# Context loads moved to ScalarE's queue, maxima planned 20 ahead instead of 12, and one LoRA slot more

## The chip, the cores and the metric

One Trainium2 chip, one of its cores. The metric is the device time of one execution in microseconds (us), lower is better. TensorE is called PE, VectorE DVE, ScalarE ACT, GpSimd POOL and SyncE SP, as in the profile's rows; PEld is PE's weight load.

## What is computed

Two cross-attention layers, one after the other, over the same context. `B` = 4 sequences, 256 query rows of width 512, 1601 context rows of width 512, 32 heads of 16.

```python
# layer 0: weights W + 2 A B (LoRA, rank 16); 8 key/value heads, each shared by 4 query heads
q = lora(x, Wq, Aq, Bq); k = lora(ctx, Wk, Ak, Bk); v = lora(ctx, Wv, Av, Bv)
attn = softmax(q @ k.T / 4); x = x + lora(attn @ v, Wo, Ao, Bo)
# layer 1: 32 key/value heads, biases, a mask over the context rows, layernorm behind
q = x @ Wq.T + bq; k = ctx @ Wk.T + bk; v = ctx @ Wv.T + bv
attn = softmax(where(mask, q @ k.T / 4, -inf)); x = x + (attn @ v) @ Wo.T + bo
out = (x - mean) / sqrt(var + 1e-5) * ln_g + ln_b
```

## The kernel before

The attention is cut into 64 **units** of four heads of one sequence: units 0 to 31 are layer 0 (8 for each sequence), 32 to 63 layer 1. One unit is scored in 13 steps of 124 context rows, each step in two halves (two heads each). A half is a matmul on PE into one of two score banks (line 929 in layer 0, 934, two matmuls, in layer 1), then an exponential on ACT (line 1028) into one of 12 places of `p_sb`. The values (line 952) are multiplied in bursts of three to five steps.

The softmax is shifted by each row's maximum, and this maximum is found *before* the scores: for each unit PE makes 32 further score chunks ("max", line 909) into a ring of three banks and DVE reduces each to one column (line 1130). `collect` joins them, PE turns them ("turn m", line 916), DVE copies them (line 1151), and SP writes them with four small DMAs as two extra rows for each half into `q_stack` (line 1398). The scores of the unit wait for these rows. With the rows in place the score matmul subtracts the maximum itself.

The keys come by way of DRAM. A k product (line 840) is read by ACT, split in two parts by POOL (1256, 1258), written to `k_dram` by SP (1361). A **stack** is then read from `k_dram` into one of three slots of `k_stack` with six DMAs of 200 KB (line 1383), in layer 1 with two more for the mask row (1389). In layer 0 two units share a stack (16 of them), in layer 1 each unit has its own (32). A stack for unit u + 2 may be read when the unit that used its slot is scored. Maxima and scores of a unit both wait for its whole stack (`stack_ready`).

The context of a sequence lies in `ctx_sb` in four chunks (three of 992 KB, one of 226 KB). When the last product that uses a chunk is done, SP loads that chunk of the next sequence (line 1302): 4 loads at the start and 28 later.

The order of everything is written out by a planner, the class `Plan`, before the instructions are made: one list of steps, which each engine goes through in order, taking the steps that are its own. The planner keeps modelled times of PE, DVE and ACT (none for DMAs). What sets the order around the change:

- `lag` says how far the maxima are behind their target, which is `LEAD` chunks ahead of the scores:

```python
lag = CHUNKS * (1 + (s + half / 2) / NT) + self.LEAD - sum(self.max_at)
rows = [h for h in (0, 1) if self.max_open(h, 2 if lag > 0 else 1)]
```

with CHUNKS = 32 and NT = 13. With lag > 0 and a free bank in the ring, a maximum goes first of all. `max_open` lets the maxima of unit u + 2 begin while u is scored only if lag > 0, its stack step has been emitted and its queries are turned ("turn q", line 897).
- `enter_unit(u)` emits what must be done before unit u: the k product of u + 2, then (once "turn m" of u is out) the step `stack` for u + 2, then the q product.
- SP's queue takes its steps in the planner's order. A step that waits holds back all behind it.
- `norm` emits one step of the layernorm for each score step: `sums`, `variance`, `root` (a square root on ACT, line 1074, which needs another function table), `centre`, `inverse`, `normalise`.

The start: LoRA factors of k and q lie in two slots (on `att_t` and `att`); those of v and o follow in the same slots when the first are used up ("fold", PE line 823, DVE 1091). `wo` and the o factors are issued by SP after the first stack.

Of the kernel before, what the change touches and what calls it, by code (L numbers as in the profile page):

```python
# [22 lines left out]
class Plan:  # L23
# [4 lines left out]
    def __init__(self, B, UB, QT, KT, NT, CT, NC, NM, CHUNKS, LEAD, RING, chunks_of_keys):  # L28
# [25 lines left out]
        self.todo, self.writes = [], []  # L54
# [39 lines left out]
    def read(self):  # L94
# [27 lines left out]
        else:  # L122
# [156 lines left out]
    def turn(self, entry):  # L279
# [37 lines left out]
    def prologue(self):  # L317
# [7 lines left out]
        self.step("load w", "wo")  # L325
        self.step("load lora", "o")
# [50 lines left out]
    def ready(self, entry):  # L377
# [88 lines left out]
    def load_stack(self):  # L466

        self.step("stack", self.next_stack)
        self.stacked, self.next_stack = self.next_stack, None

    def score(self, s, half):
        u, i = divmod(s, self.NT)
        n = 2 * s + half
        self.enter("half", half, self.score_free[n % 2])
# [6 lines left out]
        self.write_keys(s)  # L481

# [29 lines left out]
    def main(self):  # L512
        NT, CHUNKS = self.NT, self.CHUNKS
        total, s, half, places = self.UNITS * NT, 0, 0, 6
        while self.values_done < total:
# [10 lines left out]
            score_wait = max(0.0, self.score_free[(2 * s + half) % 2] - self.begins("half", half)) if score else None  # L526
# [60 lines left out]
    NORM = {"sums": 950, "variance": 200, "root": 0, "centre": 620, "inverse": 200, "normalise": 620}  # L587
# [8 lines left out]
def cross_attention_pair(nc, x, xT, ctxT, mask, w0, w1, out):  # L596
    B, S, H = x.shape
    T = ctxT.shape[2]
    P = 128
# [29 lines left out]
    LEAD = 12  # L629
# [41 lines left out]
    with ctx:  # L671
# [40 lines left out]
        lora_a = att_t[0:RANK, :, :].rearrange("p k s -> p (k s)")  # L712
        lora_b = att[0:RANK, :, :].rearrange("p q h -> p (q h)")
# [28 lines left out]
        s_w = {n: sem(f"s_w_{n}") for n in ("a0", "b0", "a1", "b1", "wq", "wk0", "wv0", "wo", "wk1", "wv1", "wq1", "wo1",  # L742
# [6 lines left out]
        s_m = [sem(f"s_m{i}") for i in range(3)]  # L749
# [14 lines left out]
        lora_slot = {"k": 0, "q": 1, "v": 0, "o": 1}  # L764
# [36 lines left out]
        def lora_loaded(e, n):  # L801
            s = lora_slot[n]
            e.wait_ge(s_w[f"a{s}"], 16 if n in "kq" else 32)
            e.wait_ge(s_w[f"b{s}"], 16 if n in "kq" else 32)
# [10 lines left out]
        def tensor(engine):  # L815
            e = Once(engine)
            for kind, *a in steps:
                if kind == "fold":
# [5 lines left out]
                                  lora_a[:, s * H + k * P:s * H + (k + 1) * P], lora_b[:, s * H:s * H + w],  # L824
# [94 lines left out]
                elif kind == "score":  # L919
# [6 lines left out]
                    e.wait_ge(s_m[u % 3], 64 * (u // 3 + 1))  # L926
# [85 lines left out]

        def scalar(engine):
            e = Once(engine)
            for kind, *a in steps:
                if kind == "score":
# [5 lines left out]
                    else:  # L1022
# [53 lines left out]
        def vector(engine):  # L1076
# [8 lines left out]
            for kind, *a in steps:  # L1085
# [32 lines left out]
                elif kind == "read turn q":  # L1118
# [4 lines left out]
                    if u >= 3:  # L1123
                        e.wait_ge(s_m[u % 3], 64 * (u // 3))
# [21 lines left out]
                elif kind == "read turn m":  # L1146
                    u, = a
                    e.wait_ge(s_made["turn m"], u + 1)
                    if u >= 2:
                        e.wait_ge(s_m[(u - 2) % 3], 64 * ((u - 2) // 3 + 1))  # L1150
# [136 lines left out]
        def sync(engine):  # L1287
            e = Once(engine)

            def load_lora(n):  # L1290
                s = lora_slot[n]
                if n in "vo":
                    e.wait_ge(s_made["fold"], fold_count["k" if n == "v" else "q"])
                engine.dma_start(lora_a[:, s * H:(s + 1) * H], w0[f"A{n}T"]).then_inc(s_w[f"a{s}"], 16)
                engine.dma_start(lora_b[:, s * H:s * H + widths[n]], w0[f"B{n}"]).then_inc(s_w[f"b{s}"], 16)

            def load_ctx(z, c):
                lo, hi = chunk(c)
                user = plan.ctx_after.get((z, c))
                if user is not None:  # L1300
                    e.wait_ge(s_made[user[0]], made[user])
# [146 lines left out]
```

## Time and profile before

| | us |
|---|---|
| median of 3 runs | 1794.33 |
| lowest, highest | 1787.55, 1794.78 |
| the profiled execution | 1788.64 |
| its span, first to last instruction | 1786.9 |
| mean granted clock of TensorE | 0.972 of full speed |

The span is the profiled execution less 1.7 us around it. Busy times are unions of an engine's instructions; on PE, where matmuls are pipelined, an interval counts as busy when any matmul is under way. A row of the form "A <- B" in a list of waits is idle time of A that ended when B finished.

### The profile page before, as it was taken

The numbers are of one execution on the slowest core, as the hardware profiler recorded it, in microseconds if no ns is written. First come the engines' busy times: TensorE is split into PE (matmuls) and PEld (weight loads), VectorE is DVE, ScalarE is ACT, GpSimd is POOL, SyncE is SP. The second block draws the span as 40 slices with busy tenths as digits, with TensorE's granted clock in tenths as the row PEclk, the third lists the DMA queues.
The fourth block names the chain that finished last, engine by engine and source line by source line (L and its number), as shares of the span: only waits on it lengthen the run. The fifth ranks groups of instructions, "written<-read, shape, count | busy, mean of one in ns | idle before, by whom it ended". The sixth has DMA issues, their size and how long they took to land.

```text
span 1786.9 us, 43754 instructions
## 1 busy us (share of the span) xinstructions
PE 1696.2 (95%) x18340; PEld 1193.5 (67%) x18340; DVE 1256.7 (70%) x2743; ACT 1022.5 (57%) x1896; POOL 176.3 (10%) x260
## 2 busy tenths in 40 slices
PE   6799999999999999999999999998999989999996
PEld 4566666676656766665667777776777677777663
DVE  2667776777758788776765776776777767777661
ACT  0056665666656666665655655665666656666554
POOL 2010121102120001121201100000000000000000
PEclk9799999999999999999999999999999999999997
DMA  8832335212353222224433444442554245344310
GB/s 203 234 81 48 66 84 151 48 32 72 84 151 66 30 48 62 63 84 125 101 42 77 85 80 106 58 58 42 104 86 57 38 64 118 44 59 58 46 25 13
DMA packets 65029, 138.12 MB, mean 77 GB/s; under 512 B 12540, under 2 KB 49436, under 8 KB 64832
## 3 DMA queue, kind: packets, MB, share of 16 engines
q1 hardware_dynamic: 64832, 135.33, 37.6%
q8 instruction: 144, 2.36, 0.6%
q14 instruction: 53, 0.43, 0.1%
HBM read 97.84 MB, written 34.89 MB: 74 GB/s over the span
## 4 chain that ended last, share of the span: by engine, by line
PE 86%; DMA 5%; DVE 3%; ACT 2%; SPq 2%; issue 1%; POOL 0%; DVEq 0%; ACTq 0%; POOLq 0%
PE value L952 21%; PE ring L909 13%; PE work L840 12%; PE work L860 11%; PE score L934 8%; PE score L929 8%; PE work L885 3%; PE work L990 3%; DMA k_stack<-k_dram 2%; PE ring L897 2%; PE work L868 1%; DVE chunk_max L1130 1%; ACT p_sb L1028 1%; DMA ctx_sb<-ctxT 1%; PE ring L962 1%
## 5 line engine op out<-in xcount | busy, mean ns | idle before, releaser
L1028 ACT ACTIVATE p_sb<-score 124x512 f32<-124x512 f32 (+1 forms) x1664 | 931.8, 598 | 639.8 <-PE score L934 317.7
L1130 DVE TENSOR_REDUCE chunk_max<-ring 128x1 f32<-128x402 f32 x2048 | 1055.8, 569 | 202.3 <-PE ring L909 187.8
L909 PE MATMUL ring<-k_stack,q_stack 64*128 64x402 f32 x2048 | 780.6, 454 | 16.3 <-DMA k_stack<-k_dram 10.5
L952 PE MATMUL value<-p_sb,v_sb 124*32 124x256 f32 x6656 | 422.5, 389 | 0.2 <-ACT p_sb L1028 0.2
L909 PEld LDWEIGHTS ring<-k_stack,q_stack 64*128 64x128 f32 x2048 | 356.9, 188 | 86.4 <-DVE chunk_max L1130 32.3
L934 PE MATMUL score<-q_stack,k_stack 64*124 64x256 f32 (+1 forms) x1664 | 362.3, 324 | 23.8 <-DMA q_stack<-few_rows 15.4
L929 PE MATMUL score<-q_stack,k_stack 64*124 64x512 f32 (+1 forms) x832 | 381.3, 503 | 1.9 <-ACT p_sb L1028 1.5
L860 PE MATMUL work<-wv,ctx_sb 64*124 64x128 f32 x3840 | 371.3, 278 | 3.1 <-issue 1.6
L860 PEld LDWEIGHTS work<-wv,ctx_sb 64*124 64x124 f32 x3840 | 341.2, 185 | 13.3 <-PE work L860 7.1
L840 PE MATMUL work<-ctx_sb,wk 64*128 64x402 f32 x1280 | 309.2, 518 | 6.2 <-DMA ctx_sb<-ctxT 4.9
L952 PEld LDWEIGHTS value<-p_sb,v_sb 124*32 124x32 f32 x6656 | 190.9, 111 | 160.7 <-issue 54.0
L934 PEld LDWEIGHTS score<-q_stack,k_stack 64*124 64x124 f32 (+1 forms) x1664 | 238.9, 184 | 79.6 <-ACT p_sb L1028 32.6
L929 PEld LDWEIGHTS score<-q_stack,k_stack 64*124 64x124 f32 (+1 forms) x832 | 144.3, 183 | 78.7 <-ACT p_sb L1028 42.7
L840 PEld LDWEIGHTS work<-ctx_sb,wk 64*128 64x128 f32 x1280 | 150.4, 189 | 31.0 <-issue 9.4
L1256 POOL CAST k_parts<-full 128x402 fp32r<-128x402 f32 x80 | 41.6, 520 | 634.8 <-ACT full L1039 623.3
L1267 POOL CAST q_nat<-full 128x512 fp32r<-128x512 f32 x32 | 19.7, 617 | 824.5 <-DVE full L1115 666.5
L885 PE MATMUL work<-wq,xt_sb 64*128 64x128 f32 x1024 | 94.3, 290 | 5.3 <-ACT v_sb L1050 2.1
L885 PEld LDWEIGHTS work<-wq,xt_sb 64*128 64x128 f32 x1024 | 81.7, 193 | 16.1 <-PE work L885 6.8
L1125 DVE CAST q_stack<-ring 128x512 fp32r<-128x512 f32 x64 | 44.0, 689 | 50.8 <-PE ring L897 48.5
L990 PE MATMUL work<-wo,att_t 64*128 64x512 f32 x256 | 77.8, 624 | 0.8 <-ACT att_t L1060 0.6
L1258 POOL TENSOR_TENSOR k_parts<-full,k_parts 128x402 fp32r<-128x402 f32 x80 | 77.3, 966 | 6.4
L1050 ACT ACTIVATE v_sb<-work 124x512 f32<-124x512 f32 (+2 forms) x100 | 38.4, 455 | 58.1 <-PE work L860 48.8
(66 smaller groups left out, 553.4 us busy)
## 6 DMA issues: line engine op xcount, KB each, us to landing
k_stack<-k_dram SPq DMA_DIRECT2D x288, 200.1 KB
k_dram<-k_parts SPq DMA_DIRECT2D x60, 402.0 KB, 2.7
ctx_sb<-ctxT SPq DMA_DIRECT2D x24, 992.0 KB, 6.9
k_dram<-k_parts SPq DMA_DIRECT2D x20, 395.0 KB, 3.3
q_stack<-few_rows SPq DMA_DIRECT2D x256, 2.0 KB
wq<-l_Wq SPq DMA_DIRECT2D x2, 1024.0 KB, 12.7
xt_sb<-xT SPq DMA_DIRECT2D x4, 512.0 KB, 13.0
wo<-l_Wo SPq DMA_DIRECT2D x2, 1024.0 KB, 9.0
```

Of the source, the lines that this page charges most:

```text
L840: done = engine.matmul(work[:, n, 0:MW], w[rows, k, col * P:(col + 1) * P], ctx_sb[rows, k, lo:lo + MW], start=(p == 0), stop=(p == 2 * KT ...
L860: done = engine.matmul(work[0:TT, n, j * P:(j + 1) * P], ctx_sb[rows, k, t0:t0 + TT], w[rows, k, col * P:(col + 1) * P], start=(p == 0), s ...
L885: done = engine.matmul(work[:, n, 0:P], xt_sb[rows, z % 2, k, n * P:(n + 1) * P], wq[rows, k, col * P:(col + 1) * P], start=(p == 0), stop ...
L909: engine.matmul(ring[bank_of["max", u, half, m]][:, 0:MW], q_stack[rows, u % 3, j, q * P:(q + 1) * P], k_stack[rows, 2 * (z % 3) + (u % 2 ...
L929: engine.matmul(score_bank[n % 2][0:tn, :], k_stack[rows, slot + u % 2, t0:t0 + tn], q_stack[rows, u % 3, :, :].rearrange("p j q -> p (j q)"),
L934: done = engine.matmul(score_bank[n % 2][0:tn, j * S:(j + 1) * S], k_stack[rows, slot + j, t0:t0 + tn], q_stack[rows, u % 3, j, :], start= ...
L952: done = engine.matmul(value_bank[32 * j:32 * j + 32, 0:S], v_sb[0:tn, seq % 2, i, head * VW:head * VW + 32], p_sb[0:tn, (2 * n + j % 2) % ...
L990: done = engine.matmul(work[:, n, :], att_t[rows, k, n * P:(n + 1) * P], wo[rows, k, :], start=(p == 0), stop=(p == 2 * KT - 1))
L1028: engine.activation(p_sb[0:tn, n % PLACES, :], score_bank[n % 2][0:tn, :], ACT.Exp, scale=SCALE).then_inc(s_exp, 1)
L1125: engine.tensor_copy(q_stack[:, u % 3, :, :].rearrange("d j q -> d (j q)"), ring[bank_of["turn q", u]][:, :]).then_inc(s_taken["turn q"], 1)
L1130: engine.tensor_reduce(chunk_max[:, u % 2, half, m // NM, m % NM:m % NM + 1], ring[bank_of["max", u, half, m]][:, 0:MW], AX.X, ALU.max)\
L1258: engine.tensor_tensor(dst[:, 1, :], one, dst[:, 0, :], ALU.subtract).then_inc(s_part, 1)
```

## The change

- **Loads of the context.** The 28 later loads are issued by ACT instead of SP, with the same wait. The planner collects them and emits them at the end of `load_stack`, or after a score when no stack is outstanding. The products on a new chunk are allowed 4 score steps after the load's step, not 2. The planner counts 450 ns of ACT for each chunk.
- **Loads of the start.** The o factors get a slot of their own in `xt_sb` (second half), and they and `wo` are issued before the constant rows and the mask; the load of `xt` 1 now waits for the fold of o.
- **Maxima.** `LEAD` is 20, not 12. The planner holds the scores of a unit back until 4.5 us after its "turn m". The semaphore of the rows is split by half: a score waits for its own half's two DMAs.
- **Root.** The step `root` comes after `centre` instead of ahead of it, and two empty steps stand between it and `inverse`.

```diff
@@ Plan.read @@
-                self.slow += [("variance", b), ("root", b)]
-                self.slow += [("centre", b, r) for r in range(self.QT)] + [("inverse", b)]
+                self.slow += [("variance", b)] + [("centre", b, r) for r in range(self.QT)]
+                self.slow += [("root", b), ("time",), ("time",), ("inverse", b)]
@@ Plan.done @@
-                    self.ctx_now[c], self.ctx_since[c] = z + 1, self.now
-                    self.step("load ctx", z + 1, c)
+                    self.ctx_now[c], self.ctx_since[c] = z + 1, None
+                    self.ctx_loads.append((z + 1, c))
+                    self.scalar_free += 450
@@ Plan.turn @@
+        if kind == "turn m":
+            self.rows_at[name[1]] = max(self.vector_free, end + self.HOP) + 4500
@@ Plan.prologue @@
-        self.step("load w", "wo")
-        self.step("load lora", "o")
@@ Plan.ready @@
-            return all(self.ctx_now[c] == z and (z == 0 or self.ctx_since[c] + 2 <= self.now) for c in chunks)
+            return all(self.ctx_now[c] == z and (z == 0 or self.ctx_since[c] is not None and self.ctx_since[c] + 4 <= self.now) for c in chunks)
@@ Plan.load_stack @@
         self.step("stack", self.next_stack)
         self.stacked, self.next_stack = self.next_stack, None
+        self.load_ctx()
+
+    def load_ctx(self):
+        for z, c in self.ctx_loads:
+            self.step("load ctx", z, c)
+            self.ctx_since[c] = self.now
+        self.ctx_loads = []
@@ Plan.score @@
-        self.enter("half", half, self.score_free[n % 2])
+        self.enter("half", half, max(self.score_free[n % 2], self.rows_at[u]))
...
         self.write_keys(s)
+        if self.next_stack is None:
+            self.load_ctx()
@@ Plan.main @@
-            score_wait = max(0.0, self.score_free[(2 * s + half) % 2] - self.begins("half", half)) if score else None
+            score_wait = max(0.0, max(self.score_free[(2 * s + half) % 2], self.rows_at[u]) -
+                             self.begins("half", half)) if score else None
@@ cross_attention_pair @@
-    LEAD = 12
+    LEAD = 20
...
+        lora_a.append(xt_sb[0:RANK, 1, 0:2, :].rearrange("p k s -> p (k s)"))
+        lora_b.append(xt_sb[0:RANK, 1, 2:4, :].rearrange("p k s -> p (k s)"))
...
-        s_m = [sem(f"s_m{i}") for i in range(3)]
+        s_m = [[sem(f"s_m{i}{half}") for half in range(2)] for i in range(3)]
...
-        lora_slot = {"k": 0, "q": 1, "v": 0, "o": 1}
+        lora_slot = {"k": 0, "q": 1, "v": 0, "o": 2}
@@ tensor, score @@
-                    e.wait_ge(s_m[u % 3], 64 * (u // 3 + 1))
+                    e.wait_ge(s_m[u % 3][half], 32 * (u // 3 + 1))
@@ scalar @@
+                elif kind == "load ctx":
+
+                    z, c = a
+                    user = plan.ctx_after[z, c]
+                    e.wait_ge(s_made[user[0]], made[user])
+                    load_ctx(engine, z, c)
@@ sync @@
             def load_xt(b):
+                if b == 1:
+                    e.wait_ge(s_made["fold"], fold_count["o"])
...
             engine.dma_start(wv0[:, :, :], by_tile(w0["Wv"])).then_inc(s_w["wv0"], 16)
+            load_lora("o")
+            engine.dma_start(wo[:, :, :], by_tile(w0["Wo"])).then_inc(s_w["wo"], 16)
             e.wait_ge(s_x_rows, X_ROWS)
```

## Rows read from the trace of the kernel before

**Rows 1.** The page: busy time (share of the span), and granted clock in 40 slices
```profile
PE 1696.2 (95%) x18340; PEld 1193.5 (67%) x18340; DVE 1256.7 (70%) x2743; ACT 1022.5 (57%) x1896; POOL 176.3 (10%) x260
...
PEclk9799999999999999999999999999999999999997
```

**Rows 2.** The waits, longest in total: who <- for whom: us, times, longest
```profile
PE score L934 <- DMA q_stack<-few_rows: 15.4, 7, 3.9
...
PE ring L909 <- DMA k_stack<-k_dram: 10.5, 3, 3.8
...
ACT rstd L1074 <- DVE rstd L1202: 6.2, 1, 6.2
...
PE work L840 <- DMA ctx_sb<-ctxT: 4.9, 3, 2.7
```

**Rows 3.** The timeline of the start: start, duration, engine, line [idle before <- releaser]
```profile
39.97 2.67 SPq L1383 DMA_DIRECT2D k_stack<-k_dram  x6
...
42.68 0.42 SPq L1338 DMA_DIRECT2D wo<-l_Wo  x1
...
55.42 7.16 PE L823 MATMUL work<-att,att_t 16*128 16x512 f32 x8 [10.32 <-DMA att<-l_Bo]
...
62.51 1.04 PE L909 MATMUL ring<-k_stack,q_stack 64*128 64x402 f32 x3
```

**Rows 4.** The timeline at the first change of sequence
```profile
289.51 1.54 SPq L1302 DMA_DIRECT2D ctx_sb<-ctxT  x3
...
293.26 4.75 SPq L1383 DMA_DIRECT2D k_stack<-k_dram  x6
...
310.63 0.67 PE L909 MATMUL ring<-k_stack,q_stack 64*128 64x402 f32 x1 [3.60 <-DMA k_stack<-k_dram]
```

**Rows 5.** Windows: length, busy PE, PEld, DVE, ACT, POOL, granted clock, DMA share, GB/s
```profile
56.00:68.00 12.00, 11.67 (x51) 6.51 (x51) 6.73 (x12) 0.00 (x0) 0.00 (x0) 0.53 1.05 387
...
300.00:310.00 10.00, 7.02 (x72) 4.44 (x68) 5.33 (x13) 3.90 (x7) 0.00 (x0) 0.98 1.05 165
...
820.00:830.00 10.00, 8.69 (x74) 5.26 (x74) 5.84 (x14) 3.97 (x7) 0.00 (x0) 0.83 0.28 92
...
1030.00:1040.00 10.00, 8.68 (x108) 6.03 (x109) 5.06 (x11) 4.42 (x10) 1.26 (x2) 1.00 0.18 35
...
1220.00:1230.00 10.00, 8.02 (x81) 7.41 (x82) 5.29 (x11) 7.44 (x11) 0.00 (x0) 0.66 0.87 125
```

**Rows 6.** The timeline of unit 55's first half: SP's stack, a burst of values
```profile
1538.70 2.65 SPq L1383 DMA_DIRECT2D k_stack<-k_dram  x6
...
1547.12 2.37 PE L952 MATMUL value<-p_sb,v_sb 124*32 124x256 f32 x40
```

**Rows 7.** Windows of one us, columns as in Rows 5: the DMA share falls to nothing
```profile
1547.00:1548.00 1.00, 1.00 (x19) 0.55 (x20) 0.99 (x3) 0.73 (x2) 0.00 (x0) 1.00 0.95 128
...
1549.00:1550.00 1.00, 1.00 (x16) 0.42 (x7) 0.11 (x1) 0.00 (x0) 0.00 (x0) 1.00 0.03 6
1550.00:1551.00 1.00, 1.00 (x15) 1.00 (x14) 0.95 (x4) 0.68 (x2) 0.00 (x0) 1.00 0.00 0
```

**Rows 8.** Maxima (line 909 alone) begun up to a time: PE's count, then PEld's
```profile
0.00:1540.10 1540.10, 694.56 (x1805) 315.90 (x1805) 0.98 0.40 83
0.00:1547.10 1547.10, 698.71 (x1818) 318.04 (x1818) 0.98 0.40 83
...
0.00:1554.30 1554.30, 701.02 (x1825) 319.17 (x1825) 0.98 0.40 83
```

**Rows 9.** The chain at unit 33's end: start, duration, what
```profile
950.50 0.37 SPq L1383
...
954.00 9.64 DMA k_stack<-few_rows
...
963.78 0.38 PE ring L909
```

**Rows 10.** The instructions that touch `ctx_sb`: ns min/median/max, first and last start
```profile
L1302 SPq DMA_DIRECT2D ctx_sb<-ctxT x32: 368/502/1905, 2.1 to 1510.2; - x32
```

**Rows 11.** The groups by line: busy us, mean ns, idle before, releaser
```profile
L1028 ACT ACTIVATE p_sb<-score 124x512 f32<-124x512 f32 (+1 forms) x1664 | 931.8, 598 | 639.8 <-PE score L934 317.7
```

More of the change, by code:

```diff
@@ L53, in __init__ @@
         self.ctx_now, self.ctx_since, self.chunk_product = [0] * NC, [0] * NC, [None] * NC
-        self.todo, self.writes = [], []
+        self.rows_at = {}
+        self.todo, self.writes, self.ctx_loads = [], [], []
         self.stacked, self.next_stack = 1, None
@@ L585, in main @@
         assert not self.todo and self.current is None
-    NORM = {"sums": 950, "variance": 200, "root": 0, "centre": 620, "inverse": 200, "normalise": 620}
+    NORM = {"sums": 950, "variance": 200, "root": 0, "time": 0, "centre": 620, "inverse": 200, "normalise": 620}
     def norm(self):
@@ L711, in cross_attention_pair @@
         rstd = sb("rstd", [P, QT])
-        lora_a = att_t[0:RANK, :, :].rearrange("p k s -> p (k s)")
-        lora_b = att[0:RANK, :, :].rearrange("p q h -> p (q h)")
+        lora_a = [att_t[0:RANK, 2 * i:2 * i + 2, :].rearrange("p k s -> p (k s)") for i in range(2)]
+        lora_b = [att[0:RANK, i, :] for i in range(2)]
+        lora_a.append(xt_sb[0:RANK, 1, 0:2, :].rearrange("p k s -> p (k s)"))
+        lora_b.append(xt_sb[0:RANK, 1, 2:4, :].rearrange("p k s -> p (k s)"))
         mask_rows = p_sb[0:B, 0:4, :].rearrange("p a n -> p (a n)")[:, 0:T].bitcast(I32)
@@ L740, in cross_attention_pair @@
         s_x_rows = sem("s_x_rows")
-        s_w = {n: sem(f"s_w_{n}") for n in ("a0", "b0", "a1", "b1", "wq", "wk0", "wv0", "wo", "wk1", "wv1", "wq1", "wo1",
+        s_w = {n: sem(f"s_w_{n}") for n in ("a0", "b0", "a1", "b1", "a2", "b2", "wq", "wk0", "wv0", "wo", "wk1", "wv1", "wq1", "wo1",
                                             "rows", "cols", "mask", "x")}
@@ L802, in lora_loaded @@
             s = lora_slot[n]
-            e.wait_ge(s_w[f"a{s}"], 16 if n in "kq" else 32)
-            e.wait_ge(s_w[f"b{s}"], 16 if n in "kq" else 32)
+            e.wait_ge(s_w[f"a{s}"], 32 if n == "v" else 16)
+            e.wait_ge(s_w[f"b{s}"], 32 if n == "v" else 16)
             e.wait_ge(s_w[{"k": "wk0", "q": "wq", "v": "wv0", "o": "wo"}[n]], 16)
@@ L823, in tensor @@
                     engine.matmul(work[:, bank_of["fold", n, k], 0:w],
-                                  lora_a[:, s * H + k * P:s * H + (k + 1) * P], lora_b[:, s * H:s * H + w],
+                                  lora_a[s][:, k * P:(k + 1) * P], lora_b[s][:, 0:w],
                                   start=True, stop=True).then_inc(s_made["fold"], 1)
@@ L1011, in tensor, with load_ctx @@
                     done.then_inc(s_made["turn mask"], 1)
+        def load_ctx(engine, z, c):
+            lo, hi = chunk(c)
+            engine.dma_start(ctx_sb[:, :, lo:hi], ctxT[z % B].rearrange("(k p) t -> p k t", p=P)[:, :, lo:hi])\
+                .then_inc(s_ctx[c], 16)
         def scalar(engine):
@@ L1123, in vector @@
                     if u >= 3:
-                        e.wait_ge(s_m[u % 3], 64 * (u // 3))
+                        for half in range(2):
+                            e.wait_ge(s_m[u % 3][half], 32 * (u // 3))
                     engine.tensor_copy(q_stack[:, u % 3, :, :].rearrange("d j q -> d (j q)"),
@@ L1149, in vector @@
                     if u >= 2:
-                        e.wait_ge(s_m[(u - 2) % 3], 64 * ((u - 2) // 3 + 1))
+                        for half in range(2):
+                            e.wait_ge(s_m[(u - 2) % 3][half], 32 * ((u - 2) // 3 + 1))
                     engine.tensor_copy(m_turned[:, u % 2, :], ring[bank_of["turn m", u]][0:2 * ROWS, 0:P])\
@@ L1291, in load_lora @@
                 s = lora_slot[n]
[L1292 to L1301, printed above, removed]
-                engine.dma_start(ctx_sb[:, :, lo:hi], ctxT[z % B].rearrange("(k p) t -> p k t", p=P)[:, :, lo:hi])\
-                    .then_inc(s_ctx[c], 16)
+                if n == "v":
+                    e.wait_ge(s_made["fold"], fold_count["k"])
+                engine.dma_start(lora_a[s], w0[f"A{n}T"]).then_inc(s_w[f"a{s}"], 16)
+                engine.dma_start(lora_b[s][:, 0:widths[n]], w0[f"B{n}"]).then_inc(s_w[f"b{s}"], 16)
             def load_xt(b):
+                if b == 1:
+                    e.wait_ge(s_made["fold"], fold_count["o"])
                 if b >= 2:
@@ L1313, in sync @@
             for c in range(NC):
-                load_ctx(0, c)
+                load_ctx(engine, 0, c)
             load_lora("q")
@@ L1336, in sync @@
                     load_lora(a[0])
-                elif kind == "load w":
-                    engine.dma_start(wo[:, :, :], by_tile(w0["Wo"])).then_inc(s_w["wo"], 16)
                 elif kind == "load layer 1":
@@ L1352, in sync @@
                     engine.dma_start(wq[:, :, :], by_tile(w1["Wq"])).then_inc(s_w["wq1"], 16)
-                elif kind == "load ctx":
-                    load_ctx(*a)
                 elif kind == "load xt":
@@ L1398, in sync @@
                             engine.dma_start(raw(q_stack[at:at + 1, u % 3, :, :]).rearrange("o j (q n) -> o (j q) n", n=P),
-                                             raw(m_turned[of:of + ROWS // 2, u % 2, :])).then_inc(s_m[u % 3], 16)
+                                             raw(m_turned[of:of + ROWS // 2, u % 2, :])).then_inc(s_m[u % 3][half], 16)
                 elif kind == "normalise":
```

## The prediction

> **What bounds the kernel now.** I read the page first: TensorE is busy for 1696 us of 1787, DVE for 70% and ACT for 57% [rows 1]. So the time is PE's work at the clock it is granted, plus PE's idle time; an edit gains only by taking idle time from PE or by sparing it a drop of the clock. Then the list of waits, for where PE idles: 10.5 us in three waits for a stack read from `k_dram`, 15.4 us in seven waits of the first score of a unit for its rows of maxima, 4.9 us for context chunks [rows 2]. Then the timeline of the start, where PE idles 10.3 us for the o factors and `wo`, issued behind the first stack [rows 3]. Last, windows around each idle stretch: after it the granted clock is at its lower level (1.2 GHz) for a while. A window of 10 us at 0.66 has lost 3.4 us of full-speed time, one at 0.83 1.7 us, and after 1.3 us of idling at 1037 us nothing was lost [rows 5]. I counted five drops of the first size and two of the second behind the waits for stacks and rows: 5 x 3.4 + 2 x 1.7 = 20.4 us.
>
> **What the change takes away.**
>
> - *Start.* `wo` and the o factors go ahead of the constant rows. The fold of o then runs right after the mask's turn at 45 us and no longer ends at 62.5. What is late next is the first stack: issued at 39.97, and a stack takes about 12 us (below), so it landed near 52; the 1 MB moved ahead of it delays SP by some 2.7 us (1 MB at the 387 GB/s that the loads behind the start reach [rows 5]), so 54.6. The first maximum began at 62.51 [rows 3]: gain 8 us. The load of `xt` 1 waits for the fold of o, but is wanted only in unit 6 or so, 150 us later: nothing. Bounds 4 and 11.
> - *Rows.* With LEAD 20 the maxima of a unit are ready 8 chunks earlier, 8/32 of a unit of some 27 us (1787 less 60 for the start, over 64) = 6.8 us. The longest wait for rows is 3.9 us [rows 2], so all 15.4 us go. The semaphore by halves then gains nothing more: the rows are there.
> - *Stacks behind the context.* At the change of sequence SP issues three chunks at 289.5, two writes, then the stack at 293.26; PE wants it at 307.0 and gets it at 310.63 [rows 4]. Three such waits, 10.5 us, plus 1.6 us in layer 1 for a stack that came behind late writes: 12.1 us.
> - *Context.* The second pair of chunks no longer stands behind a stack in SP's queue: 2.7 of the 4.9 us.
> - *Clock.* The 20.4 us above, as these waits go.
>
> Together 8 + 15.4 + 12.1 + 2.7 + 20.4 = 59 us.
>
> **What costs nothing.** The root waited for DVE once, 6.2 us, at the very end of the kernel [rows 2], where DVE's order does not change and the wait stays; in the middle it holds ACT for its two table loads wherever it stands. The empty steps issue nothing.
>
> **What it adds.**
>
> - *ACT.* 28 issues of 0.37 to 0.51 us, once 1.9 us under a full queue [rows 10]: 14 us of ACT. ACT is idle for 640 us before its exponentials, mostly waiting for PE's scores [rows 11]; this hides the most part. But an issue in front of an exponential delays the bank that the next score wants. I take 4 us; bounds 0 and 14.
> - *A new wait, for the stack.* This is the large term. A stack of layer 1 is issued when the last scores of the unit before are done, 1538.70 in unit 55's case [rows 6]; neither LEAD nor the empty queue can bring that forward. Its bytes move until 1549 to 1550 [rows 7]. Where PE waited for one, from the issue at 950.50 (or a little before) to the maximum at 963.78 it took 13 us [rows 9]; I use 12. The planner has no time for DMAs and holds a stack for ready as soon as it is emitted. Now the maxima. Unit 57's first is the 1825th, 32 x 57 + 1, and it began just ahead of 1554.3, 3.5 us after its stack landed. When unit 55 began, 1805 were out: 32 x 56 + 13, so the lead of 12 holds on the chip [rows 8]. With 20, the same place in the order is reached 8 maxima earlier, where the 1817th stood: the 1818th had begun by 1547.1 [rows 8]. By the formula of `lag` too, unit u + 2 opens 13 x (1 - 20/32) = 4.9 steps into unit u instead of 8.1. So the first maximum of 57 is issued at about 1547, ahead of the burst of values at 1547.12 [rows 6], and PE stands until 1550.5: a wait of 3.5 us. If the planner puts the burst first, 0.7 us. If "turn q" of unit u + 2 comes late (in about half of the units it is emitted only with that burst), the maximum is held back anyway and waits 0 to 2 us. I take 2 us a stack, between 0.7 and 3.5, and 25 of layer 1's 32 stacks (those that were already slack because of a wait for rows, and the last, are left out): 50 us.
> - *Layer 0.* Here a slot is free long before, and SP issues the stack right behind the rows, which come 6.8 us earlier too; nothing changes. Only the stacks behind key writes or a context load don't move: I count 7 at 2 us, 14 us. The three at the changes of sequence are among them: without the chunks ahead of it the stack would land at 293.3 + 12 = 305, and the maximum that came at 307.0 would come at about 300 were its queries turned by then.
> - *Clock again.* 32 waits of about 2 us. Waits of 1.3 to 3.6 us lost 0, 1.7 or 3.4 us each [rows 5]. I take 1.7 us for 12 of them: 20 us; bounds 0 and 54 (all at 1.7).
>
> Together 4 + 50 + 14 + 20 = 88 us.
>
> The Trainium skill bears on one point. In the windows at the change of sequence the DMA engines' share is 1.05 while only 165 GB/s move [rows 5], so a stack fills all of them. "DMA: Bandwidth & Descriptors", in "Issuing engines are not separate DMA queues", says that transfers issued by ScalarE run on the same DMA engines as SP's and interleave with them. The trace fits the first half and has no transfer from ScalarE to show the second. By that rule chunks in flight slow a stack beside them instead of standing ahead of it, and the landing at 305 would be 307 or later; that would lie inside my 2 us a stack.
>
> **The sum.** 88 - 59 = +29 us on the profiled execution's 1788.6 us: 1817.6. That execution is 5.7 us under the median of the runs but inside their range (1787.6 to 1794.8), so I keep it as the base and predict 1817 us, 1.3% above the median. Differences under 0.5%, 9 us, I count as none: 1785 to 1803.
>
> **Rivals.**
>
> 1. *The stacks come in time, and the kernel is faster.* The first maximum of u + 2 is held back by something that moves less than LEAD: the turn of its queries, a busy ring bank, the burst of values put first. For it: the 1818th maximum had begun by 1547.1 but no other by 1550.1, three microseconds in which the landing nearly catches up [rows 7, 8]. Against it: in the planner a maximum with lag > 0 goes before everything. With 32 new waits of 0.5 us and no drop of the clock: 16 + 4 - 59 = -39, and with the start at its best 1747; I put it at 1755. It decides when the new waits with their clock stay under 46 us, 1.4 us a stack.
> 2. *An even trade.* 1.6 us a stack and 8 drops: 51 + 14 + 4 - 59 = +10, or less: 1790 to 1800. For it: all terms are of one size.
> 3. *The maxima wait in full.* 3.5 us at each of 32 stacks and 1.7 us of clock for each, 166 us, + 4 - 59 = +111: 1900. Against it: the units whose queries are turned late.
> 4. *ACT becomes the wait.* If ACT's issue blocks as SP's did under a full queue, 28 x 1.9 = 53 us on ACT, of which perhaps 20 reach PE: the forecast plus 16, 1833. Its queue would hold only its own four chunks, which speaks against it.
>
> **How the numbers follow.** Forecast 0.48; rival 1 0.24; rival 2 0.18; rivals 3 and 4 0.05 each. The forecast's own range is 1803 to 1845 (1.3 to 2.7 us a stack, less or more of the clock). The range for 8 in 10 must take in both signs: 1758 to 1850. Slower by over 0.5%: the forecast, 3 and 4, 0.57. Within 0.5%: 0.19, most of rival 2. Faster: 0.24.
>
> **What the profile of the changed kernel would show.** The start: the fold of o from about 45 us, the first maximum at about 54.6. The list of waits: no `q_stack<-few_rows` on PE; and, if I am right, PE ring L909 <- DMA k_stack (from `k_dram`, or `few_rows` in layer 1, whose mask rows are issued last) some 30 times and 50 to 80 us in total, each at 5 steps into a unit. Fewer than 10 such waits, or under 20 us, and the forecast is wrong and rival 1 right. The page's PEclk row would have more 9s turned to 8s in layer 1. DMA queues: a second hardware queue with the chunks. ACT's table loads for the root stay. The prediction falls if the planner's order, with its new times, puts bursts or products in front of the first maximum of u + 2; that I could only judge from the order before.

## The result, and the profile after

The changed kernel takes 1832.53 us (median of 4 runs, 1826.42 to 1834.03), the kernel before 1794.55 beside it: a ratio of 1.0211, 95% interval 1.0173 to 1.0249, so slower by 2.1%. The forecast was 1817 us and slower, within a range of 1758 to 1850.

The page after, the parts that answer to [rows 1], with the DMA queues and the start of the chain that ended last:

```profile
PE 1708.1 (93%) x18340; PEld 1208.7 (66%) x18340; DVE 1257.8 (69%) x2743; ACT 1022.5 (56%) x1896; POOL 175.8 (10%) x260
...
PEclk8799999999999999999998999989999999999988
...
q1 hardware_dynamic: 50048, 112.38, 32.0%
q10 hardware_dynamic: 14784, 22.95, 4.3%
...
PE 78%; DMA 12%; SPq 4%; ACT 2%; DVE 2%; issue 1%; POOL 0%; ACTq 0%; DVEq 0%; POOLq 0%
```

The span is 1832.0 us and the mean granted clock 0.961, against 1786.9 and 0.972. The same 18340 matmuls keep PE busy for 12 us more, and PE is idle for 1832.0 - 1708.1 = 123.9 us instead of 90.7. The two 8s in the middle of the PEclk row stand in slices with long waits for a stack; the 8s at its ends are the start and the end of the kernel. DMA has 12% of the chain, where it had 5%. The new queue q10 carries the context chunks issued by ACT.

The list of waits after, which answers to [rows 2] (line 924 is the old 909, line 1100 the old 1074):

```profile
PE ring L924 <- DMA k_stack<-few_rows: 55.2, 19, 7.7
PE ring L924 <- DMA k_stack<-k_dram: 15.2, 3, 5.9
...
ACT rstd L1100 <- DVE rstd L1230: 6.2, 1, 6.2
...
PE work L855 <- DMA ctx_sb<-ctxT: 2.0, 1, 2.0
```

The waits of the scores for their rows (15.4 us in seven) are gone. In their place the first maximum of a unit waits for its stack: 70.4 us in 22 waits, where it was 12.1 in four.

The timeline after, at units 33 and 41, each with SP's stack and the first maximum that needs it (35 x 32 = 1120 maxima had begun by 967.7, 43 x 32 = 1376 by 1197.5, so these are the first of units 35 and 43; line 1403 is the old 1383):

```profile
952.97 1.78 SPq L1381 DMA_DIRECT2D k_dram<-k_parts  x2
954.80 3.06 SPq L1403 DMA_DIRECT2D k_stack<-k_dram  x6
957.90 1.23 SPq L1409 DMA_DIRECT2D k_stack<-few_rows  x2
967.83 0.71 PE L924 MATMUL ring<-k_stack,q_stack 64*128 64x402 f32 x2 [6.88 <-DMA k_stack<-few_rows]
...
1185.51 2.65 SPq L1403 DMA_DIRECT2D k_stack<-k_dram  x6
...
1197.64 0.67 PE L924 MATMUL ring<-k_stack,q_stack 64*128 64x402 f32 x1 [3.58 <-DMA k_stack<-few_rows]
```

From SP's issue to the maximum 12.1 us pass at the second, 13.0 at the first, as in [rows 9]. The wait is the part of this in which PE had nothing else in front: 3.58 us for a plain stack, and 6.88 where two key writes stand before the stack in SP's queue. Nine waits of 3.3 us and more hold 43.9 of the 55.2 us. The 22 maxima that waited came 11.6 to 13.0 us after their stack's issue in 18 cases (median 11.9) and 17.2 to 17.9 us after it in four; beside those four, context chunks were in flight.

The chain for the longest wait, at unit 45's first steps:

```profile
1301.13 0.31 SPq L1403
...
1304.63 13.51 DMA k_stack<-few_rows
...
1318.28 0.67 PE ring L924
```

Here the stack needs 17.1 us. ACT issued two context chunks of 992 KB at 1300.78 and 1301.19, just as SP began with it. Windows after, behind such waits (columns as in [rows 5]):

```profile
894.00:914.00 20.00, 15.20 (x184) 11.66 (x174) 8.56 (x22) 6.82 (x13) 0.00 (x0) 0.83 0.27 33
958.00:978.00 20.00, 13.12 (x151) 9.57 (x153) 7.12 (x19) 4.25 (x8) 0.00 (x0) 0.74 0.38 48
...
1192.00:1212.00 20.00, 16.42 (x176) 11.05 (x173) 10.15 (x25) 8.19 (x18) 0.00 (x0) 0.83 0.18 23
1223.00:1243.00 20.00, 16.74 (x172) 11.40 (x169) 12.17 (x29) 8.47 (x16) 0.00 (x0) 0.91 0.20 25
```

After each of the nine long waits the clock is at its lower level (1.2 GHz) for a stretch. In such windows of 20 us, one around each, the granted clock is 0.83 six times (20 x 0.17 = 3.4 us lost), 0.91 twice (1.8) and 0.74 once (5.2): 29 us together. By the intervals of the clock in the trace, 7 of the 29 us fell while PE still stood in the wait, the rest on matmuls behind it.

The start after, which answers to [rows 3], and the first change of sequence, [rows 4]:

```profile
43.18 2.67 SPq L1403 DMA_DIRECT2D k_stack<-k_dram  x6
...
49.04 0.59 PE L1024 MATMUL ring<-ident,p_sb 13*124 13x13 f32 x4 [1.60 <-DVE p_sb L1124]
49.48 7.17 PE L838 MATMUL work<-xt_sb 16*128 16x512 f32 x8
...
56.58 1.04 PE L924 MATMUL ring<-k_stack,q_stack 64*128 64x402 f32 x3
...
282.32 0.53 ACTq L1030 DMA_DIRECT2D ctx_sb<-ctxT  x1
...
285.31 3.06 SPq L1403 DMA_DIRECT2D k_stack<-k_dram  x6
...
303.16 0.70 PE L924 MATMUL ring<-k_stack,q_stack 64*128 64x402 f32 x2 [4.22 <-DMA k_stack<-k_dram]
```

### The profile page after: what moved, and what is told of

It is laid out like the page before. It is cut to its first block, busy times and chain, and to the rows that moved or that the text cites. A ratio compares the mean times of both kernels' runs of the same rounds, so it can differ in the third digit from the quotient of the medians.

```text
span 1832.0 us, 43837 instructions
## 1 busy us (share of the span) xinstructions
PE 1708.1 (93%) x18340; PEld 1208.7 (66%) x18340; DVE 1257.8 (69%) x2743; ACT 1022.5 (56%) x1896; POOL 175.8 (10%) x260
## 4 chain that ended last, share of the span: by engine, by line
PE 78%; DMA 12%; SPq 4%; ACT 2%; DVE 2%; issue 1%; POOL 0%; ACTq 0%; DVEq 0%; POOLq 0%
PE value L967 19%; PE ring L924 12%; PE work L855 12%; PE work L875 10%; DMA k_stack<-few_rows 9%; PE score L944 8%; PE score L949 6%; PE work L900 3%; SPq L1403 3%; PE work L1005 2%; DMA k_stack<-k_dram 2%; PE work L883 2%; PE ring L912 1%; ACT p_sb L1048 1%; PE ring L977 1%
## 5 line engine op out<-in xcount | busy, mean ns | idle before, releaser
L924 PE MATMUL ring<-k_stack,q_stack 64*128 64x402 f32 x2048 | 784.1, 460 | 76.9 <-DMA k_stack<-few_rows 55.2
L967 PE MATMUL value<-p_sb,v_sb 124*32 124x256 f32 x6656 | 433.3, 395 | 0.4 <-ACT p_sb L1048 0.4
L875 PE MATMUL work<-wv,ctx_sb 64*124 64x128 f32 x3840 | 376.9, 279 | 1.1
L944 PE MATMUL score<-q_stack,k_stack 64*124 64x512 f32 (+1 forms) x832 | 374.3, 502 | 3.1 <-ACT p_sb L1048 2.5
L949 PE MATMUL score<-q_stack,k_stack 64*124 64x256 f32 (+1 forms) x1664 | 357.0, 318 | 11.0 <-ACT p_sb L1048 10.4
L855 PE MATMUL work<-ctx_sb,wk 64*128 64x402 f32 x1280 | 303.7, 516 | 3.2 <-DMA ctx_sb<-ctxT 2.0
L1152 DVE CAST q_stack<-ring 128x512 fp32r<-128x512 f32 x64 | 44.1, 690 | 52.1 <-PE ring L912 49.9
```

Source lines behind the costliest of these rows:

```text
L855: done = engine.matmul(work[:, n, 0:MW], w[rows, k, col * P:(col + 1) * P], ctx_sb[rows, k, lo:lo + MW], start=(p == 0), stop=(p == 2 * KT ...
L875: done = engine.matmul(work[0:TT, n, j * P:(j + 1) * P], ctx_sb[rows, k, t0:t0 + TT], w[rows, k, col * P:(col + 1) * P], start=(p == 0), s ...
L924: engine.matmul(ring[bank_of["max", u, half, m]][:, 0:MW], q_stack[rows, u % 3, j, q * P:(q + 1) * P], k_stack[rows, 2 * (z % 3) + (u % 2 ...
L944: engine.matmul(score_bank[n % 2][0:tn, :], k_stack[rows, slot + u % 2, t0:t0 + tn], q_stack[rows, u % 3, :, :].rearrange("p j q -> p (j q)"),
L949: done = engine.matmul(score_bank[n % 2][0:tn, j * S:(j + 1) * S], k_stack[rows, slot + j, t0:t0 + tn], q_stack[rows, u % 3, j, :], start= ...
L967: done = engine.matmul(value_bank[32 * j:32 * j + 32, 0:S], v_sb[0:tn, seq % 2, i, head * VW:head * VW + 32], p_sb[0:tn, (2 * n + j % 2) % ...
```

## The experiments

Each ratio is to runs of the kernel before on the same chip; these had medians of 1788 to 1795 us. "Stack waits" are PE's waits for `k_stack` in the list of waits; "idle" is the span less PE's busy time; "clock" is (1 - mean granted clock) x span, both of the one profiled execution; "planned" is the median time from a stack's step to the unit's first maximum in the planner's own times. The clock's loss varies between executions of one kernel: in 43 of the kernel before it was 44 to 72 us (median 59), in the four of the changed kernel 62 to 71 (median 68). So a difference of 10 us in the clock's column tells nothing by itself, and the 50.0 of the kernel before is at the low side.

| kernel | planned | stack waits | idle | clock | us | ratio, 95% |
|---|---|---|---|---|---|---|
| before | 15.4 | 12.1 (4) | 90.7 | 50.0 | 1794.55 | 1 |
| changed | 11.1 | 70.4 (22) | 123.9 | 71.4 | 1832.53 | 1.0211 [1.0173, 1.0249] |
| changed, LEAD 12 | 15.7 | 10.4 (4) | 66.8 | 29.8 | 1762.41 | 0.9841 [0.9799, 0.9884] |
| changed, LEAD 15 | 13.4 | 24.8 (8) | 75.5 | 37.3 | 1785.91 | 0.9964 [0.9936, 0.9993] |
| before, LEAD 20 | | 80.2 (27) | 141.6 | 70.2 | 1849.23 | 1.0326 [1.0277, 1.0375] |
| changed, short stacks | 11.1 | 17.9 (10) | 73.7 | 37.0 | 1759.37 | 0.9830 [0.9798, 0.9863] |
| changed, planner told | 13.1 | 22.0 (8) | 71.2 | 42.5 | 1770.76 | 0.9905 [0.9880, 0.9931] |
| changed, chunks by SP | 11.1 | 64.3 (22) | 128.3 | 67.8 | 1835.85 | 1.0258 [1.0220, 1.0295] |
| changed, LEAD 12, chunks late | | 10.8 (4) | 79.2 | 47.9 | 1774.38 | 0.9927 [0.9900, 0.9954] |
| before, start alone | 15.4 | 9.3 (4) | 74.4 | 56.8 | 1784.85 | 0.9975 [0.9953, 0.9996] |
| before, chunks by ACT | 15.4 | 3.2 (3) | 82.6 | 42.6 | 1780.00 | 0.9960 [0.9937, 0.9983] |
| before, rows' plan | | 8.9 (3) | 67.6 | 35.1 | 1756.99 | 0.9836 [0.9811, 0.9861] |
| before, the three | 15.9 | 1.8 (2) | 63.6 | 29.7 | 1753.30 | 0.9815 [0.9783, 0.9846] |
| the three, LEAD 14 | 14.1 | 10.4 (6) | 75.7 | 40.6 | 1768.88 | 0.9888 [0.9857, 0.9920] |

**LEAD taken back, and LEAD alone.** Two kernels: `LEAD = 12` in the changed one, and `LEAD = 20` in the kernel before.

> The changed kernel with LEAD back at 12, all else kept. My theory (maxima planned 20 ahead come to a stack before it has landed): the waits of PE for k_stack fall from 70 us in 22 to under 12 us, the clock drops behind them go, and with the start's 8 us and the planner's wait for the rows kept the time is 1755 to 1775 us. Rival (the loss comes from ACT issuing the context's loads, or from the planner holding scores and products back): LEAD gives back little, 1810 us or more.

> The kernel before with LEAD 20 and nothing else. My theory: the waits for the rows of maxima (15 us) go, some 20 new waits for k_stack come, 60 us and more with the three at the changes of sequence, and the time is 1825 to 1850 us, above even the changed kernel, since the start's gain is missing. Rival (the loss needs the other edits): at most 1795 us.

The waits with LEAD 12 in the changed kernel, then with LEAD 20 in the kernel before:

```profile
PE ring L924 <- DMA k_stack<-k_dram: 10.4, 4, 3.6
...
PE score L944 <- DMA q_stack<-few_rows: 1.2, 1, 1.2
```
```profile
PE ring L909 <- DMA k_stack<-few_rows: 54.1, 21, 6.7
PE ring L909 <- DMA k_stack<-k_dram: 26.1, 6, 6.7
```

Both came out as expected. LEAD turns a gain of 1.6% into a loss of 2.1%, and alone costs 3.3%. In the first pair LEAD is the only difference, and no other wait of PE for a transfer changed by more than 1.2 us.

**Short stacks.** If the wait is for bytes, fewer bytes must shorten it, with LEAD left at 20. From the fourth stack on, this kernel issues 4 of a stack's 6 loads. The last third of its rows isn't read again, so that part of each product with the keys is computed from an earlier stack's.

```diff
-                    for r, part in KPARTS:
+                    for r, part in (KPARTS if z < 3 else KPARTS[0:2]):
```

> The changed kernel, LEAD 20, but from the fourth stack on only four of its six DMAs are issued (the second copy of the keys' upper part is left as it was, so the scores lack a small correction). The order of all engines is the same. A stack then lands about 3.5 us sooner (a third of 10 us of transfer). My theory: the waits for k_stack of 1 to 4 us go almost all, the four long ones of 6 to 8 us shrink to 3 or 4, together from 70 to 20 us or less, and the time is 1765 to 1790 us. Rival (the waits named k_stack only stand for another lag, as the queries' turn or DVE): the time falls by less than 10 us.

```profile
PE ring L924 <- DMA k_stack<-few_rows: 13.0, 7, 4.5
...
PE ring L924 <- DMA k_stack<-k_dram: 4.9, 3, 2.3
```

The order of the instructions is the changed kernel's, and the waits fall from 70.4 to 17.9 us, by 52.5. The time falls by 73 us, to 1759, just under the 1765 to 1790 that I expected. In the profiled spans, 72.3 us apart, 50.2 are idle time of PE and 23.7 are clock lost while PE was busy (53.7 and 30.0 us). The whole loss of the clock differs by 71.4 - 37.0 = 34.4 us; what of it falls in PE's idle time is idle time already.

**The planner told of the landing.** Loads and LEAD as in the changed kernel; the planner takes a stack as landed 12.5 us after its step and puts no maximum of that unit before it.

```diff
@@ Plan.load_stack @@
+        self.stack_at[self.next_stack] = max(self.free) + 12500
@@ Plan.maximum @@
-        self.enter("half", half, self.ring_free[bank])
+        self.enter("half", half, max(self.ring_free[bank], self.arrives(unit)))
```

> The changed kernel with LEAD 20 as it is, but the planner is told that a stack has landed 12.5 us after its step, and emits no maximum of the unit (and sets the time of none) before that, doing other work instead. Nothing else is changed; DMAs and their count are those of the changed kernel. Theory: LEAD 20 costs only through maxima that stand at the head of PE's queue before their stack is there; with them held back in the plan, the waits for few_rows fall from 55 to under 15 us and the time to 1760 to 1785. Rival: PE has nothing else to do in that time (scores held by ACT), so the idle time comes back under another name, p_sb or ring, and the time stays above 1810.

```profile
PE ring L930 <- DMA k_stack<-k_dram: 16.8, 5, 5.0
...
PE ring L930 <- DMA k_stack<-few_rows: 5.2, 3, 2.3
```

The waits for `few_rows` fell from 55.2 to 5.2 us and did not return under another name: idle time is 71.2 us. So PE had other work to put in front. The `k_dram` waits stayed; three of the five are at the changes of sequence, where PE had the stack 16.9 to 17.5 us after its issue, while the planner is told 12.5.

**Dose.** LEAD 15 in the changed kernel, with the two kernels of three edits further down.

> The changed kernel with LEAD 15, between the 12 and the 20 that were measured (1762 and 1832). In the planner's times the first maximum follows its stack's step by at least 9.5 us (median 13.4). Theory: the wait opens when this falls under about 12 us, so a part of the stacks is waited for, 10 to 25 us of waits for few_rows, time 1770 to 1795. Rival, that the time goes with LEAD in a straight line for another reason: 1762 + 70 x 3/8 = 1788 with hardly any waits for the stack.

```profile
PE ring L924 <- DMA k_stack<-k_dram: 17.1, 5, 4.7
PE ring L924 <- DMA k_stack<-few_rows: 7.7, 3, 3.9
```

The time fits both theories, the waits only the first: 24.8 us of them. But most are in layer 0 (`k_dram`), where I had expected `few_rows`. Waits of 10.4, 24.8 and 70.4 us at LEAD 12, 15 and 20 go with a planned distance of 15.7, 13.4 and 11.1 us, against the 11.6 to 13.0 us (17.2 to 17.9 beside context chunks) that a waited-for stack took in the changed kernel. With LEAD 15, 11.5 of the 24.8 us are at the three changes of sequence.

**Who issues the chunks.** In the changed kernel the 28 loads go back to SP at the places of the plan; in the kernel before they go to ACT at their old places.

> The changed kernel with the 28 later context loads issued by SP again, at the same place in the planner's order (behind the stack). If ACT's issues cost PE what I estimated, 4 us is gained; SP's queue then holds rows or stacks back by 0.5 us each, so the same time within 10 us: 1825 to 1840. Rival (ACT's issues are a large part of the loss): 1810 or less. Rival (a queue of its own is what keeps the stacks from being worse): 1845 or more.

> The kernel before with the 28 later context loads issued by ScalarE at the same places in the planner's order, nothing else. My reading: the stack at a change of sequence no longer stands behind three chunks in SP's queue but shares the DMA engines with them, so the three waits of 3.6 us shrink but do not go, and ACT's issues cost up to 4 us: the time is lower by 0 to 10 us. Rival (the queue was the cause): the three waits go wholly, 20 us with their clock. Rival (ACT's issues cost PE time): slower by 5 us or more.

The first changed nothing in the time that can be told, but two terms under it moved, against each other. At 97 us PE waits 9.8 us for a chunk, since all four now stand behind the second stack in SP's queue; the waits at the changes of sequence shrink from 15.2 to 11.0 us:

```profile
PE work L855 <- DMA ctx_sb<-ctxT: 12.0, 2, 9.8
```

The `few_rows` waits are 53.3 us in 19. The longest is again at unit 45, with the chunks issued by SP just ahead of the stack:

```profile
1304.89 2.97 SPq L1402 DMA_DIRECT2D k_stack<-k_dram  x6
...
1321.67 0.67 PE L924 MATMUL ring<-k_stack,q_stack 64*128 64x402 f32 x1 [7.80 <-DMA k_stack<-few_rows]
```

That is 16.8 us from issue to use, against 17.1 with ACT as the issuer. The Trainium skill, "DMA: Bandwidth & Descriptors", section "Issuing engines are not separate DMA queues", says that transfers of all issuers share the same DMA engines and interleave; the two figures agree. At the changes of sequence the issuer shows a little: PE had the stack 17.2 to 17.9 us after its issue with ACT as the chunks' issuer and 15.4 to 16.7 with SP, and the chunk issued last before the first of these stacks took 20.3 us instead of 9.1. In the kernel before, with its plan kept, the move helped a little, 0.4%:

```profile
PE ring L909 <- DMA k_stack<-k_dram: 1.9, 2, 1.2
```

There 10.5 us of waits became 1.9, where I had expected them to shrink less:

```profile
288.08 1.49 ACTq L1015 DMA_DIRECT2D ctx_sb<-ctxT  x3
...
290.75 0.94 PE L885 MATMUL work<-wq,xt_sb 64*128 64x128 f32 x12 [1.33 <-ACT full L1049]
...
293.79 3.65 SPq L1383 DMA_DIRECT2D k_stack<-k_dram  x6
...
308.27 0.41 PE L909 MATMUL ring<-k_stack,q_stack 64*128 64x402 f32 x1 [1.17 <-DMA k_stack<-k_dram]
```

The stack was not issued earlier than in [rows 4]; the last of the three chunks was issued 4.7 us before it instead of 2.7, and the stack took 14.5 us instead of 17.4. ACT's issues have a price here: they stand in front of ACT's reading of a product, and PE waits for ACT at each of the three changes of sequence, 3.8 us in all. In the changed kernel none shows: PE's waits for `p_sb` are 10.4 us in 11 with either issuer.

**Chunks kept away from a stack.** Since two chunks beside a stack cost it 5 us, I held them until five steps after a stack's step, with LEAD 12; they are no longer issued right behind a stack either.

```diff
-        if self.next_stack is None:
+        if self.next_stack is None and (s < 5 or s >= self.stack_now + 5):
             self.load_ctx()
```

> The changed kernel with LEAD 12, with the context's loads held back until five score steps (about 10 us) after a stack's step, so that a chunk is not in flight with a stack. If sharing the DMA engines is what leaves the 10 us of waits for k_stack in the run with LEAD 12, they fall to under 3 us and the time is 5 to 15 us under that run's: 1748 to 1757 us. Rival (those waits come from the key writes and the queries' load beside the stack, or from the late issue): no difference, 1762 within 4.

```profile
PE score L943 <- ACT p_sb L1047: 7.1, 7, 5.9
...
PE work L854 <- DMA ctx_sb<-ctxT: 5.5, 2, 3.4
```

The time came out against my reading: the stack waits stayed (10.8 us in four), new waits for chunks and for ACT opened, and it is 12 us slower than LEAD 12 alone. But the edit does not do what it was made for. It holds a chunk back behind the last stack, not ahead of the next one, and there nothing moved:

```profile
289.36 0.93 ACTq L1029 DMA_DIRECT2D ctx_sb<-ctxT  x2
...
290.32 0.53 ACTq L1029 DMA_DIRECT2D ctx_sb<-ctxT  x1
...
293.45 3.76 SPq L1402 DMA_DIRECT2D k_stack<-k_dram  x6
...
310.76 0.70 PE L923 MATMUL ring<-k_stack,q_stack 64*128 64x402 f32 x2 [3.44 <-DMA k_stack<-k_dram]
```

The last chunk goes out 3.1 us before the stack, as with LEAD 12 alone, and the stack takes 17.3 us. So this run does not tell whether chunks in flight make these waits.

**The start alone.** The kernel before with the o factors' slot and the early loads.

> The kernel before with the loads of the start alone (wo and the o factors ahead of the constant rows, in a slot of their own). My term for it was a gain of 8 us, bounds 4 and 11. In the changed kernel the first maximum began about 6 us earlier, so 6 to 8 us: a ratio of 0.9955 to 0.9965. Rival (the gain is given back, since a DMA that starts earlier delays the first stacks or the context of the second sequence): no difference, within 3 us.

The first maximum began at 56.39 instead of 62.51, but the ratio shows only 0.25%, under the 0.35 to 0.45% that I expected, with an interval that reaches from 0.04 to 0.47%. In all traces the first maximum comes at 61.3 to 62.5 us with the old start and at 54.1 to 57.4 with the new one.

**The rows' plan alone.** The kernel before, LEAD 12, and only the planner's hold of 4.5 us behind "turn m".

```diff
+        if kind == "turn m":
+            self.rows_at[name[1]] = max(self.vector_free, end + self.HOP) + 4500
...
-        self.enter("half", half, self.score_free[n % 2])
+        self.enter("half", half, max(self.score_free[n % 2], self.rows_at[u]))
```

> The kernel before with one edit of the planner: the scores of a unit are held back until 4.5 us after its turn of the maxima, so that other work is put there. LEAD stays 12, the semaphore stays whole. My reading after the first runs: this alone takes the 15 us of waits for the rows and their clock drops (12 us) away, 1765 to 1775 us on a base of 1790. Rival (the work that fills the wait is missing later; the planner's own total grows by 5 us): 1780 or more. Rival (the maxima's lead is what takes the waits): no gain.

```profile
PE ring L913 <- DMA k_stack<-k_dram: 8.9, 3, 4.3
```

No wait for rows is left, at LEAD 12. This edit alone gives 1.6%, more than I expected (1757 us, not 1765 to 1775) and as much as the whole changed kernel with LEAD 12.

**The three together, and LEAD 14.** Rows' plan, start and chunks by ACT in the kernel before; then the same with LEAD 14.

> The kernel before with three edits that were measured alone: the planner holds a unit's scores until 4.5 us after its turn m, wo and the o factors are loaded first at the start, and the context is loaded from ACT at the places where SP loaded it. LEAD stays 12, the root stays where it was. Alone they gave ratios of 0.9836, 0.9975 and 0.9960. My theory (each removes another wait: rows, start, stacks at a change of sequence) lets them add up: 0.977, about 1748 us, with waits for k_stack under 5 us. The rival is that with the rows' wait gone PE comes to the changes of sequence at another point and the waits there open again, or that clock lost in one place is lost in another: then 1755 or more, no better than the plan of the rows alone.

> The same with LEAD 14. In the planner's times the first maximum of a unit then follows its stack's step by at least 11.5 us (median 14.1) instead of 12.8 (15.9). A stack takes about 12 us, so my theory expects almost no new waits: within 0.3% of the one with LEAD 12, at most 5 us of waits for few_rows. A rival in which LEAD itself costs, by more turmoil in the order of maxima and scores, expects 5 us or more above it without such waits.

PE's waits for transfers with LEAD 12, then the stack waits with LEAD 14:

```profile
PE work L827 <- DMA wk<-l_Wk: 4.8, 1, 4.8
...
PE score L938 <- DMA q_stack<-few_rows: 2.3, 1, 2.3
...
PE ring L913 <- DMA k_stack<-k_dram: 1.5, 1, 1.5
```
```profile
PE ring L913 <- DMA k_stack<-k_dram: 9.1, 5, 2.5
...
PE ring L913 <- DMA k_stack<-few_rows: 1.3, 1, 1.3
```

The three give 0.9815, the lowest ratio of the study, but its interval overlaps that of the rows' plan alone (0.9836), and the full sum of 0.977 was not reached. The waits named are nearly gone (1.8 us for stacks, one of 2.3 for rows), 7.5 us of the start too, yet the idle time fell from 67.6 to 63.6 us only: others opened, among them again three for ACT at the changes of sequence (4.0 us). Whether the three add at all stays open. LEAD 14 costs 0.7% and brings 8.6 us more of stack waits, nearly all in layer 0. I had expected almost none: I set about 12 us beside the shortest planned distance, 11.5 us, while PE had the six waited-for stacks 12.4 to 15.3 us after their issue. The idle time grew by 12.1 us.

## Why the prediction was right, and where it was mis-sized

**The mechanism was right.** A maximum planned 20 ahead of the scores stands at the head of PE's queue before its stack has landed. Taking LEAD back removes the waits, LEAD alone makes them, fewer bytes shorten them, and telling the planner of the landing avoids most of them, at the same LEAD.

**The size of the stack term.** I took 25 x 2 + 7 x 2 = 64 us. Measured are 70.4, so 58 net of the old 12.1, where I had 52; the waits are 22, not some 30. The sum is close, its parts are not. In layer 1 there are 19 waits of 2.9 us instead of 25 of 2: the longer plain ones are at my upper bound of 3.5 us (3.26 to 3.84), three behind key writes exceed it (4.80, 6.34, 6.88), as does the one beside context chunks (7.72), and 20 of the 32 units have about 1 us or none. Unit 57 itself, on which I worked out 3.5 us, waits 0.93. In layer 0 only the three changes of sequence wait, 5.1 us each; four of the seven that I counted don't.

**The changes of sequence.** I priced 12.1 us as gone and took 6 of them back as new waits. In fact they grew from 10.5 to 15.2 us. Moving the chunks to ACT did not take their bytes out of the stack's way: at the first one the stack was issued at 285.31, 8 us earlier than in [rows 4], but PE had it only at 303.16, 17.9 us later, where I had counted 12. In [rows 4] 17.4 us pass, so the stack is hardly slower than before; with LEAD 20 its first maximum is due sooner after the issue. Of the two readings that I set side by side there, the traces favour chunks in flight that slow a stack, at 5 us and more where I allowed 2: where PE waited for such a stack, 16.8 to 17.9 us passed from issue to use with the last chunk 2.7 to 3.1 us ahead (the kernel before and the changed one), 13.8 to 15.3 us with it 4.7 ahead (the chunks by ACT at their old places). No run kept the chunks away to show it.

**The clock.** This is the term that was mis-sized most. I let 20.4 us go and put 20 us back, a change of nothing: 1.7 us for 12 of 32 waits. In the trace the clock falls at 14 of the 22 waits and loses 43 us, 3 each; the nine long waits of layer 1 alone lost 29 us. Over the whole profiled executions the loss went from 50.0 to 71.4 us, 21 more; between the medians of the executions (59 and 68) it is only 9 more, so how much of the 21 belongs to the change stays open. The profiled execution that I took as the base lost less than most and is 5.7 us under the median: from median to median the change is +38, where I had +29.

**The start.** I said 8 us; the first maximum came 5.9 earlier (56.58 for 62.51). The wait of 10.3 us is gone, but more than the first stack (3.2 us) came later: the turn of the mask moved from 44.51 to 49.04 (from 46.0 to 47.0 in the other three traces with the old start, to 46.2 to 49.9 with the new one), and the fold of o, 7.2 us long, stands between it and the first maximum. The stack is not what is late next; the fold is.

**What held.** All 15.4 us for the rows went. But I gave LEAD the credit and had no term for the planner's hold of 4.5 us. Either one removes them: none is left with LEAD 20 alone, none with the hold alone, 1.2 us in the changed kernel with LEAD 12. So LEAD 20 bought nothing that the hold had not. The context's waits went from 4.9 to 2.0 us. ACT's issues, put at 4 us, cost nothing that the comparison of issuers in the changed kernel shows; in the kernel before, at their old places, they brought 3.8 us of waits. The 6.2 us wait at the root stayed.

**The sum from measured terms.** Stack waits +58.3, rows -15.4, context -2.9, start -5.9, clock +21.4: +55.5, against +45.1 in the spans. These terms are not apart from each other: clock lost while PE stands in a wait costs nothing more. Parted so that nothing counts twice, the 45.1 us are +33.2 idle time of PE, +16.5 clock lost while PE was busy (37.2 to 53.7), and -4.6 in PE's busy time otherwise, which no run explains.

**Not tried.** The root's new place and the rows' semaphore by halves were not run alone, nor was a kernel in which no chunk goes out in the microseconds ahead of a stack. With LEAD 12 the whole changed kernel and the rows' plan alone are equal within their intervals, so together with the start and ACT they bring nothing that these runs can tell.

## What to carry to other kernels

A planner that has no time for transfers will place their first reader too early as soon as its look-ahead grows; compare, for each load, the planned distance from issue to first use with the time that the load took in the trace, and take the longest time for loads in the same company: here 13.0 us for a plain stack, 17.9 beside context chunks. If one wait is due to work planned too early, first try to move that work (here the scores, held 4.5 us: 1.6%), before a look-ahead is changed that shifts everything. Price the clock with each wait: here nine waits of 3.3 to 7.7 us, 43.9 us together, went with 29 us of lost clock, 22 of them on top of the waits.

## What was not expected of the hardware

- In the changed kernel PE had a waited-for stack of 1.2 MB 11.6 to 13.0 us after its issue, and after 17 us or more with 2 MB and more of context issued up to 3 us ahead of it. Who issued the context made 0.4 us of difference at unit 45 and 0.5 to 2.3 us at the changes of sequence.
- How far ahead the context was issued matters more: in the kernel before 2 us more of it (4.7 instead of 2.7) took 2.9 us off the stack at the first change of sequence.
- The clock's share of a loss is large: between the changed kernel and the one whose planner was told of the landing, stack waits differ by 48.4 us and the clock's loss by 28.9 (27 between the medians of four executions each), with the same loads and nearly the same matmuls' busy time (1698.5 against 1708.1 us).
